# Order of the first keys, their copies and the warm-up products in a cross-attention kernel on one Trainium2 core

## The reference

```python
def _L0_xattn_ref(q, k, v, Wq, bq, Wk, bk, Wv, bv):    # q = layernorm(x), k = v = ctx_1024
    qp = jnp.einsum('bsd,ed->bse', q, Wq) + bq         # 256 x 128
    kp = jnp.einsum('bsd,ed->bse', k, Wk) + bk         # 25088 x 128
    vp = jnp.einsum('bsd,ed->bse', v, Wv) + bv
    z = jnp.einsum('bqe,bke->bqk', qp, kp)
    z = jax.nn.sigmoid(z / scale)                      # no softmax
    return jnp.einsum('bqk,bkd->bqd', z, vp)
```

## Time and profile before

| | us |
|---|---|
| median of 3 executions | 571.96 |
| lowest, highest | 571.60, 572.12 |
| the profiled execution | 571.72 |
| its span, first to last instruction | 569.9 |
| TensorE busy in it | 563.5 (99%) |
| VectorE busy | 463.0 (81%) |
| ScalarE busy | 405.4 (71%) |
| GpSimd busy | 1.7 |
| mean granted clock of TensorE | 0.999 |

### The profile page before, as it was taken

How to read it: one execution, slowest core, us unless ns; L and a number is a source line. 1 busy time by engine, 2 the same in 40 slices (tenths; PEclk the granted TensorE clock), 3 DMA queues, 4 the chain that set the end, 5 groups by cost and what they waited for, 6 DMA issues and landing times.

```text
span 569.9 us, 8034 instructions
## 1 busy us (share of the span) xinstructions
PE 563.5 (99%) x2967; PEld 473.9 (83%) x2967; DVE 463.0 (81%) x520; ACT 405.4 (71%) x558; POOL 1.7 (0%) x7
## 2 busy tenths in 40 slices
PE   8999999999999999999999999999999999999998
PEld 5888888888888888888888888888888888787886
DVE  6987878787878898888879888978787879898685
ACT  6876768677777777777777777777676776599350
POOL 1000000000000000000000000000000000000000
PEclk9999999999999999999999999999999999999999
DMA  8668787877777777877787778676788663100201
GB/s 334 221 206 239 237 244 233 233 216 244 216 227 253 258 239 232 266 231 237 251 265 237 235 242 266 206 225 215 224 272 234 214 194 132 38 1 2 75 0 37
DMA packets 33239, 115.88 MB, mean 203 GB/s; under 512 B 4081, under 2 KB 4785, under 8 KB 32945
## 3 DMA queue, kind: packets, MB, share of 16 engines
q1 hardware_dynamic: 32768, 115.05, 63.7%
q10 hardware_dynamic: 432, 0.33, 0.2%
HBM read 114.84 MB, written 0.52 MB: 202 GB/s over the span
## 4 chain that ended last, share of the span: by engine, by line
PE 96%; DVE 1%; ACT 1%; DMA 1%; issue 0%; DVEq 0%
PE ps L1016 94%; ACT w L573 1%; PE ps L1280 1%; DMA x_s<-in_x 1%; PE ps L1110 0%; DVE sm_s L857 0%; DVE st L696 0%; PE ps L1296 0%; DVE st L770 0%; DVE aTs L880 0%; DVE x_s L768 0%; PE ps L1249 0%; DVE h_s L786 0%; DVE h_s L711 0%; DVE o_s L977 0%
## 5 line engine op out<-in xcount | busy, mean ns | idle before, releaser
L1016 PE MATMUL ps<-nh,zh 128*128 128x512 f32 x388 | 142.7, 390 | 0.0
L1016 PE MATMUL ps<-nl,zh 128*128 128x512 f32 x388 | 142.6, 389 | 0.0
L1016 PE MATMUL ps<-nh,zl 128*128 128x512 f32 x388 | 142.5, 389 | 0.0
L679 DVE TENSOR_TENSOR zl<-zf,zh 128x1024 fp32r<-128x1024 f32 x49 | 60.1, 1226 | 80.2 <-ACT zh L402 80.2
L669 DVE TENSOR_TENSOR nl<-rawn,nh 128x1024 fp32r<-128x1024 f32 x96 | 113.9, 1221 | 1.4 <-issue 1.1
L658 DVE TENSOR_TENSOR tl<-rawt,th 128x1024 fp32r<-128x1024 f32 x96 | 113.2, 1218 | 0.0
L402 ACT ACTIVATE nh<-rawn 128x1024 fp32r<-128x1024 f32 x96 | 100.6, 1059 | 11.8 <-DMA rawn<-in_ctxn 10.4
L402 ACT ACTIVATE th<-rawt 128x1024 fp32r<-128x1024 f32 x96 | 96.6, 1054 | 1.6 <-DMA rawt<-in_ctxt 1.6
L433 ACT ACTIVATE zf<-ps 128x512 f32<-128x512 f32 x98 | 58.2, 597 | 54.2 <-PE ps L1016 48.4
L1016 PEld LDWEIGHTS ps<-nl,zh 128*128 128x128 f32 x388 | 72.8, 188 | 15.2
L1016 PEld LDWEIGHTS ps<-nh,zl 128*128 128x128 f32 x388 | 72.8, 188 | 15.1
(11 more groups left out here) (188 smaller groups left out, 611.5 us busy)
## 6 DMA issues: line engine op xcount, KB each, us to landing
rawn<-in_ctxn SPq DMA_DIRECT2D x97, 512.0 KB, 6.7
rawt<-in_ctxt SPq DMA_DIRECT2D x96, 512.0 KB, 4.9
h_s<-in_wg SPq DMA_DIRECT2D x4, 512.0 KB, 7.4
h_s<-in_wu SPq DMA_DIRECT2D x4, 512.0 KB, 6.4
wds<-in_wd SPq DMA_DIRECT2D x4, 512.0 KB, 3.9
raw<-in_ctxt SPq DMA_DIRECT2D x2, 512.0 KB, 8.0
h_s<-in_wvt SPq DMA_DIRECT2D x2, 512.0 KB, 7.5
wq_s<-in_wq SPq DMA_DIRECT2D x1, 1024.0 KB, 9.5
```

The costliest lines, as they stand in the source:

```text
L679: e.tensor_tensor(zl[b % 2][:], zf[:], zh[b % 2][:], ALU.subtract).then_inc(*s.zl.mark(b))
L1016: return e.matmul(o, w, x, start=start, stop=stop)
```

## The change

Six edits, all in the stretch ahead of the loop:

1. load_t(0, 0) becomes two transfers of 256 KB each (QUARTERS), with a semaphore each.
2. ScalarE's copy th(0, 0) becomes two copies of 128 x 512, the first with the new semaphore thq.
3. wkl is made by GpSimd, after its memsets, and no longer by VectorE.
4. There are 12 warm-up products, not 17.
5. The four keys (0, 0, 0), (0, 1, 0), (0, 0, 1), (0, 1, 1) stand ahead of the transposes; the other four with i = 0, 1 behind them.
6. In weights(0) the first half copy zh stands between the two sigmoids.

```diff
             for r in range(2):
                 e.dma_start(x_s[:, r, :], xr[:, r, :]).then_inc(*s.dx[r].mark("x"))
-            load_t(0, 0)
+            e.dma_start(rawt[:, QUARTERS[0]], ctxt[0][:, QUARTERS[0]]).then_inc(*s.dtq.mark("t"))
+            e.dma_start(rawt[:, QUARTERS[1]], ctxt[0][:, QUARTERS[1]]).then_inc(*s.dt[0].mark(0))
             load_t(0, 1)
...
             e.memset(one_s[:], 1.0).then_inc(*s.pz.mark("one"))
+            e.wait_ge(*s.wkh.of("w"))
+            e.tensor_tensor(wkl[:], wk_s[:], wkh[:], ALU.subtract).then_inc(*s.wkl.mark("w"))
...
                     e.activation(zf[:, gs], bank(2 + g), ACT.Sigmoid, scale=SC).then_inc(*s.zf.mark((b, g)))
-                if b == 0:
-                    e.wait_ge(*s.zf.of((0, 0)))
-                    copy(zh[0][:, 0:512], zf[:, 0:512]).then_inc(*s.zh0.mark("zh"))
+                    if b == 0 and g == 0:
+                        e.wait_ge(*s.zf.of((0, 0)))
+                        copy(zh[0][:, 0:512], zf[:, 0:512]).then_inc(*s.zh0.mark("zh"))
                 e.wait_ge(*s.zf.of((b, 1)))
...
             e.activation(stat(18), mv[:, :, 1], ACT.Sqrt, bias=eps_s[:]).then_inc(*s.lnq.mark("first"))
-            split_t(0, 0)
+            e.wait_ge(*s.dtq.of("t"))
+            copy(th[:, QUARTERS[0]], rawt[:, QUARTERS[0]]).then_inc(*s.thq.mark("t"))
+            e.wait_ge(*t_landed(0, 0).of(0))
+            copy(th[:, QUARTERS[1]], rawt[:, QUARTERS[1]]).then_inc(*s.th.mark((0, 0)))
             split_t(0, 1)
...
-            e.wait_ge(*s.wkh.of("w"))
-            e.tensor_tensor(wkl[:], wk_s[:], wkh[:], ALU.subtract).then_inc(*s.wkl.mark("w"))
             split_t(0, 0)
...
             e.wait_ge(*s.wz.of("wz"))
-            for _ in range(17):
+            for _ in range(12):
                 mm(bank(7), wz[:, 0:P], wz[:], True, True)
+            e.wait_ge(*s.wkh.of("w"))
+            e.wait_ge(*s.thq.of("t"))
+            key(0, 0, 0)
+            e.wait_ge(*s.wkl.of("w"))
+            key(0, 1, 0)
+            e.wait_ge(*s.th.of((0, 0)))
+            key(0, 0, 1)
+            key(0, 1, 1).then_inc(*s.kw.mark(0))
             e.wait_ge(*s.did.of("w"))
             for r in range(2):
                 e.wait_ge(*s.lnh.of(("first", r)))
                 transposes(h_s, r, 6 + r).then_inc(*s.lnt.mark(("first", r)))
-            e.wait_ge(*s.wkh.of("w"))
-            for k in range(2):
-                e.wait_ge(*s.th.of((0, k)))
-                for c in (2 * k, 2 * k + 1):
-                    key(0, 0, c)
-                if k == 0:
-                    e.wait_ge(*s.wkl.of("w"))
-                for c in (2 * k, 2 * k + 1):
-                    m = key(0, 1, c)
-                m.then_inc(*s.kw.mark(k))
+            e.wait_ge(*s.th.of((0, 1)))
+            for i, c in ((0, 2), (0, 3), (1, 2), (1, 3)):
+                m = key(0, i, c)
+            m.then_inc(*s.kw.mark(1))
             e.wait_ge(*s.tl.of((0, 0)))
```

More of the change, by code:

```diff
@@ L20 @@
 HALF = (slice(0, TILE // 2), slice(TILE // 2, TILE))
+QUARTERS = (slice(0, TILE // 4), slice(TILE // 4, TILE // 2))
 UNITS = [(0, list(range(8))), (1, list(range(4))), (0, list(range(8, 16)))] + \
@@ L92, in signals @@
     s.zh, s.zl, s.za = (steps(n, tiles) for n in ("zh", "zl", "za"))
+    s.dtq, s.thq = steps("dtq", ["t"], 16), steps("thq", ["t"])
     s.zh0 = steps("zh0", ["zh"])
@@ L653, in split_t @@
                 n = HALF[k]
+                if (b, k) == (0, 0):
+                    e.wait_ge(*s.thq.of("t"))
+                    e.wait_ge(*s.dtq.of("t"))
                 e.wait_ge(*t_landed(b, k).of(b))
```

## The result

| us | before | after |
|---|---|---|
| median of 14 executions each | 571.87 | 572.51 |
| lowest, highest | 571.58, 572.20 | 571.93, 574.03 |
| the profiled execution | 571.72 | 573.64 |
| its span | 569.9 | 571.8 |
| mean granted clock in it | 0.999 | 0.997 |

The kernel before is measured again here, beside the changed one; its median of 14 takes the place of the 571.96 of three. The ratio is 1.0016, with a 95% interval of 1.0009 to 1.0024: the changed kernel is slower by 0.5 to 1.4 us, where 0.2 us less was forecast. The kernel before spreads over 0.6 us, the changed one over 2.1, and its executions fall in two groups: nine with a mean granted clock of 1.000, at 571.93 to 572.98 (median 572.32), and five with 0.997, at 573.42 to 574.03 (median 573.89). The profiled one is of the second group.

The account below looks back on a forecast made before the run. TensorE was taken as the bound, busy 563.5 of 569.9 us, so only the loop's starting point could move. A win of 0.48 us less 0.29 given back made -0.19, forecast 571.8 us, range 571.1 to 572.9.

Parts of the forecast that it names:

- The win of 0.48 us: Ahead of the loop: the next four keys start at 9.22 us instead of 9.70, bounded by th(0, 1)'s copy and transfer.
- the DMA engines are behind with their work, so I take 0: Block 0's loads: SyncE's extra transfer delays nothing behind it; without the backlog, 0.45 us on th(0, 1).
- The first key, GpSimd and VectorE: Start of the kernel: first key at 7.21 us; wkl on GpSimd takes 1.2 us, cost 0; VectorE loses 0.69 us of work.
- Keys ahead of the transposes: TensorE before the loop: four keys from 7.21, transposes 8.20 to 9.06, next keys at 9.22 instead of 9.70, 0.48 us won.
- Sigmoid, copy, sigmoid, copy: weights(0): the sequence takes 2.41 us instead of 2.12; idle 0.27 goes, a zl wait of about 0.55 comes, giving back 0.29.
- Rival C: Warm-up: with 12 products the clock doesn't rise in time, keys and transposes run slow, 1.5 us late, 573.3 us; chance 0.16.
- Rival B: Keys ahead of the transposes: GpSimd's late wkl holds up key (0, 1, 0); a 3.5 us subtraction gives 572.8; chance 0.07.
- The sum: Start of the loop: -0.48 + 0.29 = -0.19 us, which put on the median gives 571.8 us.

Follow-up runs that it names:

- b_split: Kernel before, first half of block 0 loaded in two transfers of 256 KB cut by columns, one copy waiting for both: 572.48 us, ratio 1.0013.
- a_17: Changed kernel with 17 warm-up products instead of 12: 572.63 us, ratio 1.0013 to the kernel before.
- a_one_17: Changed kernel with one transfer for the first half and 17 warm-up products: 571.86 us, ratio 1.0001 to the kernel before.
- b_pool: Kernel before with only wkl's subtraction moved from VectorE to GpSimd: 571.73 us, ratio 1.0000.
- a_one_17_old: Changed kernel with one first-half transfer, 17 warm-up products and the old order sigmoid, sigmoid, copy, copy: 571.58 us, ratio 0.9998 to the kernel before.
- b_12: Kernel before with 12 warm-up products instead of 17: 571.97 us, ratio 1.0011; 5 of 11 executions at 573.03 to 573.28.
- b_hold: Kernel before, SyncE waiting for block 0's first half to land before issuing load_n(0, 0) and the loads behind it: 572.48 us, ratio 1.0015.

## Why the prediction was wrong

- **The win of 0.48 us rested on landings that the change itself moved.** The step that failed is "the DMA engines are behind with their work, so I take 0" for the extra transfer. I named the other end myself, 0.45 us on th(0, 1); the measured slip is 1.10 us there (8.16 to 9.26) and 0.9 to 1.1 for the second quarter. In time it costs 0.75 us (b_split) or 0.77 (a_17 against a_one_17: 572.63 and 571.86, from two series in which the kernel before lies 0.03 apart). Why the slip is larger than the 0.45 us of one issue stays open.
- **The first key, GpSimd and VectorE** went as forecast: key at 7.24 (7.21), wkl in 1.26 us (1.2, between 0.48 and 1.44), at no cost (b_pool 571.73 against 571.73).
- **Keys ahead of the transposes**: with the transfer whole, 17 products and the old order, this part and GpSimd's together give 0.12 us, not 0.48, and even that is within the noise. The step was right in its form (the keys move into idle time), but its gain needed the data at 7.21. In a_one_17_old, with the half landed at 7.1, the four keys run from 7.88 and the transposes from 8.88; the loads of the next keys start at 9.65, where they started at 9.70, and those of the query projection 0.17 earlier than the 11.08 of the earlier trace rows:
```profile
10.91 1.71 PEld L1023 LDWEIGHTS ps<-hT,zf 128*128 128x128 f32 x8
```
  In this order the transposes wait for the first half's transfer, its copy and the four keys, where they had waited for h_s alone: the change put the data on the path that it was meant to shorten.
- **Sigmoid, copy, sigmoid, copy**: right in mechanism and size. Give-back 0.29 forecast; 0.29 in the traces, 0.28 and 0.24 in the medians. The wait of about 0.55 us for zl is 0.53.
- **Rival C, the clock, is what made the executions of the upper group.** Twelve products instead of 17 bring it, by b_12. Its price is 1.5 to 1.9 us in about four executions of ten (5 of 14, 5 of 11, 5 of 11), where I had said 1.5; in all kernels with 17 products it is none. The form is only partly known. I let the clock fail to rise; in the changed kernel's trace it rose near 5.4 us and fell at 8.7, after TensorE had had two products in 2.6 us. But of the fifteen executions with a mean clock of 0.997 only this one was traced. In b_12's trace the rise came behind the warm-up, and in two of the thirteen traces with 17 products, b_hold and b_split, behind 6.4 us, where twelve slow products would have ended, so my form may lie behind some of the others. My argument against C, that the old kernel had such a hole too, compared 0.57 us of idle time with a hole that is 0.8 at best and, with the quarter late, two holes of 1.22 and 0.72 us. I gave C 0.16 as if one clock state would hold for all executions; it is a mixture, which moves the median a little and the mean more. The pace of the warm-up products changes near 5.4 us in the changed kernel's trace and near 6.1 in that of the kernel before, near 4.2 in b_pool's and near 7.3 in b_split's:
```profile
1.31 6.81 PE L1023 MATMUL ps<-wz 128*128 128x512 bf16 x17 [1.31 <-POOL wz L398]
```
  The Trainium skill (TensorE: Matmul & The Clock Gate, "What you observe") states that the rise comes at another time from run to run, by about half a microsecond either way. The traces agree that it moves, and they spread wider, over some 3 us.
- **Rival B's price** was added up wrong: a subtraction of 3.5 us would end at 8.83, 1.23 behind the slack at 7.60, which gives 573.0 and not 572.8. Nothing in the forecast hangs on it.
- **The sum, redone with measured terms**, on the kernel before's 571.7: -0.12 (keys and GpSimd), +0.28 (order), +0.77 (cut) give 572.6, as a_17 has by construction; with 12 products the executions at the full clock lie at 572.32, and a third of them 1.5 us higher. Why those at the full clock are 0.3 below a_17 I haven't tested; the two are from different series.

## What to carry to other kernels

Idle time behind a warm-up does not make its last products free: here 17 instead of 12 took the executions with the slow clock from 15 of 36 to none. Count products off only after looking at the spread of ten executions or so, because one trace shows one of the two states; whether the later products serve to raise the clock or to keep it up isn't settled here. A transfer cut in two wasn't free while the DMA engines had work waiting: before moving consumers up to meet the first piece, measure the cut by itself, with what it does to everything behind it. And where a chain of dependent pairs (sigmoid, copy) replaces two independent runs on one engine, add the time that overlap was hiding, and ask who needs the last piece rather than the first.

## What was unexpected in the hardware

- With one transfer more for the same bytes on SyncE's queue the copies of the data started 0.6 to 1.8 us later in the traces, with 4 KB rows as with 2 KB rows, and the medians rose by 0.50 to 1.07 us. With the extra one issued from ScalarE's queue the copies were still 0.5 us late, but the median rose by only 0.16.
- While GpSimd subtracts two tiles in SBUF, a tiny operation of VectorE with a single input waits for it: the one on st (128 x 2) takes 0.43 us instead of 0.17 and ends at 6.71, 0.03 after GpSimd's subtraction (5.42 + 1.26 = 6.68); in b_pool it ends 0.02 after (6.71 and 6.69). It was hidden here behind ScalarE's square root. The Trainium skill (SBUF — State Buffer, "Who interferes with whom") lists tensor_scalar among the operations that can take the shared port pair and then block; the trace agrees.
- The granted clock reads 1.00 during the slow warm-up products but 0.50 in the later fall, although the pace shows 1.2 GHz in both (0.42 us for 512 columns; eight transposes in 1.91 us and not 1.07).
- In b_12's trace the clock rose while TensorE was idle, between 6.6 and 8.0 us, behind a warm-up of which every product had run at the slow pace.
